# A cross-attention kernel: weights loaded to other buffers, and the work of the first part in another order

## The reference, cut to what matters

```
q    = heads(x @ W_q)                       # x: 4 x 2048 x 640, 20 heads of 32
k, v = heads(text @ W_k), heads(text @ W_v) # text: 4 x 73 x 1024
out  = softmax(q k^T * s) v
k_ip, v_ip = heads(ip @ W_k_ip), heads(ip @ W_v_ip)  # ip: 4 x 4 x 1024
sem  = <l2norm(probs @ text), l2norm(ip)>
out += (softmax(q k_ip^T * s + 0.5 * sem) * mask) v_ip
out  = out @ W_out + b_out + x
```

## Time and profile before

| | |
|---|---|
| median of three runs | 1020.25 us |
| profiled execution, whole | 1022.47 us |
| its span, first to last instruction | 1020.6 us |
| first part, to the barrier | 0 to 88.7 us |
| main loop | 88.7 to 1020.6 us |
| PE busy in the span | 969.2 us (95%) |
| DVE, ACT, POOL busy | 816.6, 695.6, 655.2 us |
| DMA, mean | 177 GB/s |

### The profile page before, as it was taken

One profiled execution on the slowest core, in us unless ns is written; L12 is line 12 of the kernel. 1 busy time (PEld: TensorE's weight loads), 2 busy tenths in 40 slices (PEclk: granted clock), 3 DMA queues, 4 the chain that ended last, 5 costly groups with the idle time before them and its releaser, 6 DMA issues.

```text
span 1020.6 us, 24929 instructions
## 1 busy us (share of the span) xinstructions
PE 969.2 (95%) x7684; PEld 803.6 (79%) x7684; DVE 816.6 (80%) x2409; ACT 695.6 (68%) x2332; POOL 655.2 (64%) x1906
## 2 busy tenths in 40 slices
PE   5987788999999999999999999999999999999988
PEld 5875666888878888888887888888878888888855
DVE  6685698888888887888888888878878888878872
ACT  3534887777776777767776777777667777777740
POOL 3224587776676667677766777676667767776761
PEclk9978999999999999999999999999999999999999
DMA  9936999989889998899899989998899989887973
GB/s 293 298 117 161 195 179 186 177 163 180 168 186 186 186 185 177 163 176 162 174 178 192 192 164 191 169 167 173 167 190 187 180 169 190 137 157 154 149 138 111
DMA packets 488147, 180.27 MB, mean 177 GB/s; under 512 B 449694, under 2 KB 467155, under 8 KB 488015
## 3 DMA queue, kind: packets, MB, share of 16 engines
q1 hardware_dynamic: 487983, 178.63, 86.3%
q10 hardware_dynamic: 32, 0.07, 0.0%
HBM read 42.34 MB, written 27.22 MB: 68 GB/s over the span
## 4 chain that ended last, share of the span: by engine, by line
PE 77%; DMA 5%; DVE 4%; ACT 2%; issue 2%; SPq 2%; POOL 1%; DVEq 0%; ACTq 0%; POOLq 0%
PE ps_O L1257 25%; PE ps_Q L1368 25%; PE ps_S L1278 12%; PE ps_U L1354 11%; DMA pts<-ph 4%; PE ps_M L1294 3%; ACT pr L1038 2%; DMA x_in<-in_x_dram 1%; SPq L951 1%; DVE pr L1199 0%; PE ps_U L1257 0%; DVE n L1211 0%; ACT ph L1050 0%; DVE bias L1160 0%; SPq L924 0%
## 5 line engine op out<-in xcount | busy, mean ns | idle before, releaser
L1038 ACT ACTIVATE pr<-ps_S,bias 128x73 f32<-128x73 f32 x1280 | 288.8, 339 | 101.3 <-DVE bias L1160 100.1
L1120 POOL TENSOR_TENSOR ph<-pr,ph 128x220 f16<-128x220 f32 (+1 forms) x640 | 274.0, 460 | 126.2 <-ACT ph L1050 126.2
L1368 PE MATMUL ps_Q<-xT,wq_hi 128*128 128x512 f32 x800 | 280.1, 415 | 5.2 <-DVE qT L1127 5.2
L1257 PE MATMUL ps_O<-wo_hi,aT 128*128 128x320 f16 x1220 | 279.2, 300 | 0.0
L1050 ACT ACTIVATE ph<-pr 128x292 f16<-128x292 f32 x640 | 241.2, 500 | 0.0
L1257 PE MATMUL ps_O<-wo_lo,aT 128*128 128x320 f16 x610 | 182.3, 299 | 0.0
L1354 PE MATMUL ps_U<-xm,pts 128*128 128x110 f16 (+1 forms) x2560 | 159.3, 212 | 14.9 <-DMA pts<-ph 13.5
L1368 PEld LDWEIGHTS ps_Q<-xT,wq_hi 128*128 128x128 f32 x800 | 146.2, 191 | 32.7 <-DVE qT L1127 6.5
L1354 PEld LDWEIGHTS ps_U<-xm,pts 128*128 128x128 f16 (+1 forms) x2560 | 144.4, 98 | 32.3 <-issue 11.8
L1278 PE MATMUL ps_S<-kbd,qT 128*128 128x308 f32 x960 | 163.0, 304 | 2.6 <-ACT pr L1038 2.1
L1278 PEld LDWEIGHTS ps_S<-kbd,qT 128*128 128x128 f32 x960 | 150.8, 188 | 18.6 <-issue 3.0
(11 more groups left out here) (228 smaller groups left out, 1338.9 us busy)
## 6 DMA issues: line engine op xcount, KB each, us to landing
out_dram<-x_in SPq DMA_DIRECT2D x64, 320.0 KB, 2.6
x_in<-in_x_dram SPq DMA_DIRECT2D x56, 320.0 KB, 3.2
pts<-ph SPq DMA_TRANSPOSE x320, 3.4
w_k<-in_L_xattn_W_k_dram SPq DMA_DIRECT2D x5, 512.0 KB, 8.8
w_ip<-in_L_xattn_W_k_ip_dram SPq DMA_DIRECT2D x1, 2560.0 KB, 11.0
w_v<-in_L_xattn_W_v_dram SPq DMA_DIRECT2D x5, 512.0 KB, 8.3
w_ip<-in_L_xattn_W_v_ip_dram SPq DMA_DIRECT2D x1, 2560.0 KB, 10.6
x_in<-in_x_dram SPq DMA_DIRECT2D x2, 1280.0 KB, 7.2
```

The source lines that it names most:

```text
L1038: last = nc.scalar.activation(pr[p % P_RING][:, j, h, :], sc[:, j, h, 0:T], ACT.Exp, bias=bias[p % 2][:, j, h:h + 1], scale=SCALE)
L1120: nc.gpsimd.tensor_tensor(lo, full[:, :, t0:t1], one[:, :, 0, t0:t1], ALU.subtract).then_inc(pl_ready, 1)
L1257: last = nc.tensor.matmul(bank[:, 0:HALF], stationary, moving, start=(k, a, b_) == O_MMS[0], stop=(k, a, b_) == O_MMS[-1])
L1368: last = nc.tensor.matmul(ps_Q[:], wq[a][:, c, k * P:(k + 1) * P], xT[(CC * i + c) % XT_RING][b_][:], start=(c, a, b_) == Q_MMS[0], stop=( ...
```

## The change

W_q is loaded to a buffer of its own, `w_q`, that lies in the place of `wq_lo`, so that `wq_lo` is computed in place. `w_raw` is then free, and W_out is loaded to it right behind the bias and the mask, with no wait. `ctx_sum` moves from the place of `wq_lo` to the place of the loaded context, `x_in`, and so POOL may only write it once the context's maximum has been taken: the `partition_all_reduce` of that maximum now stands ahead of it. The rest is order.

```diff
-        ctx_sum = nc.alloc_sbuf_tensor_at("ctx_sum", [P, EC, B, T_ALL], F32, offset=g["wq_lo_at"])
+        ctx_sum = g["late0"][:, 0:EC * B * T_ALL].rearrange("p (c b t) -> p c b t", c=EC, b=B)
+        w_q = nc.alloc_sbuf_tensor_at("w_q", [P, CC, C], F32, offset=g["wq_lo_at"])
...
-                sp.dma_start(w_raw[:], g["W_q"].rearrange("(c p) n -> p c n", p=P)).then_inc(ld_wq, 16)
+                sp.dma_start(w_q[:], g["W_q"].rearrange("(c p) n -> p c n", p=P)).then_inc(ld_wq, 16)
...
+                sp.dma_start(w_raw[:], g["W_out"].rearrange("(c p) n -> p c n", p=P)).then_inc(ld_wo, 16)
...
-                sp.wait_ge(wq_hi, 1)
-                sp.wait_ge(wq_lo, 1)
-                sp.dma_start(w_raw[:], g["W_out"].rearrange("(c p) n -> p c n", p=P)).then_inc(ld_wo, 16)
```

More of the change, by code:

```diff
@@ L327, in _ @@
                         key_weights(c + 2)
+                    if c == CC - 2:
+                        act.wait_ge(ld_wq, 16)
+                        nc.scalar.activation(wq[0][:], w_q[:], ACT.Copy).then_inc(wq_hi, 1)
                 value_weights(0)
@@ L339, in _ @@
                                      ACT.Copy).then_inc(k_hi, 1)
[L340 to L345, removed]
                 def value_columns(m):
@@ L364, in value_words @@
                                          ACT.Copy, scale=ss[0:B * GI, 12:13]).then_inc(vw_hi, 1)
+                value_weights(2)
                 value_columns(0)
+                for b in range(B):
+                    act.wait_ge(kg_ready, b + 1)
+                    nc.scalar.activation(kg_raw[:, b, :], ps_S[b % 2][0:T, 0:T_ALL], ACT.Copy).then_inc(kg_read, 1)
+                    if b + 3 < CC:
+                        value_weights(b + 3)
                 act.wait_ge(kg16_ready, 1)
@@ L552, in _ @@
                 link(nc.vector.tensor_scalar(ss[:, 28:29], ss[:, 18:19], 2.0 / 2 ** 14, None, ALU.mult))
+                value_weights(3)
+                value_weights(4)
+                value_max(1)
+                v.wait_ge(vip_parts, 2)
+                nc.vector.tensor_copy(parts[1][:, HALF:C], ps_parts[1][:, 0:HALF]).then_inc(vip_copied, 1)
+                v.wait_ge(wo_hi, 1)
+                nc.vector.scalar_tensor_tensor(out=wo[1][:], in0=w_raw[:], scalar=ss[:, 11:12], in1=wo[0][:],
+                                               op0=ALU.mult, op1=ALU.subtract).then_inc(wo_lo, 1)
+                value_max(2)
                 v.wait_ge(vipt_ready, 1)
@@ L592, in _ @@
                 nc.vector.tensor_scalar(ss[:, 10:11], ss[:, 7:8], float(2 ** 14), ss[:, 24:25], ALU.mult, ALU.min).then_inc(scaled, 1)
-                for n in range(8, 2 * CC):
+                for n in range(4, 2 * CC):
                     words_lo(n)
@@ L682, in _ @@
                 last.then_inc(k_ready, 1)
+                pe.wait_ge(k_lo, CC)
+                values(0)
                 pe.wait_ge(ipt_read, 1)
@@ L705, in _ @@
                 values(3)
+                values(4)
                 pe.wait_ge(vip_read, HG)
@@ L708, in _ @@
                 pe.wait_ge(ld_wo, 16)
-                for n in range(4):
-                    value_words(n)
-                values(4)
-                for n in range(4, 2 * CC):
+                for n in range(2 * CC):
                     value_words(n)
```

66 lines of the change are left out of this document (29 added, 37 removed).

## The result

The changed kernel took **1032.76 us** (median of four runs, 1031.56 to 1033.5) where the kernel before took 1019.5 on the same chip (1017.63 to 1022.09): ratio **1.012**, 95% interval 1.0105 to 1.0135. The forecast was 1014.5 us, and the range ended at 1018.2. The change is slower, and the prediction is wrong in sign. The profiled execution of the changed kernel took 1033.39 us, its span 1031.6, and its barrier fell at 97.8 instead of the forecast 82.9 (88.7 less the gain of 5.8).

The account below looks back on a forecast made before the run. PE's first part, up to the barrier at 88.7 us, was taken to bound the gain, the main loop being unchanged. 5.2 us to the `parts` copy plus 0.6 from the fold on made 5.8: 1020.25 - 5.8 = 1014.5 us, range 1011.8 to 1018.2.

Parts of the forecast that it names:

- stage B: From the context's maximum to the second `parts` copy: `ctx_sum` 33.5 to 39.0, `wv_lo(0)` held 3.1 us, gain 5.2 us.
- my DVE chain: DVE's work from the sum's end at 39.0 to the second `parts` copy: 18.4 us, ending at 57.4, before 62.63.
- the fourth rival: At the late sum on POOL: small scale operations and the PSUM copy on DVE also stand; 1016.2 us, chance 0.08.
- The turns of DVE and POOL: During POOL's eight copies, DVE goes between two ready POOL instructions; waiting for one copy costs 0.5 us.
- POOL didn't keep its turn: Denies the rival that POOL keeps its turn through the eight copies: DVE 3.5 us later, 1018.0 us, chance 0.07.
- Stage A: Up to the context's maximum: `ctx_sum` no longer beside `wk_lo`; PE gains 2.5 us, the maximum comes 1.7 us sooner.
- W_out early: W_out issued at about 33, there by 41, wanted at 45; W_v_ip lands by 50; nothing charged.
- one pause of 2.6: PE's wait before the fold, from about 54.8 to 57.4; the low clock behind it was charged 1.5 us.
- the pause of 4.35 us: PE's wait for the `parts` copy in the kernel before, 58.3 to 62.7; forecast to shrink to 2.6 us.
- the clock doesn't fall: Rival behind PE's pause before the fold: no low clock, or only inside the pause; 1.5 us more gain, 1013.0, chance 0.15.
- The slower rival: From PE's stop at 55 to the barrier the clock stays low: 1030 us, chance 0.04.
- loss 1: In the kernel before, PE waits 1.88 us for a `wk_lo` that stood until POOL's `ctx_sum` was done.

Follow-up runs that it names:

- e1: Changed kernel with the context's sum made by DVE, behind its copy of the first parts, instead of by POOL: 1013.5 us, ratio 0.9926 to the kernel before.
- e2: Changed kernel with the three all-reduces of bias, mask and W_out ahead of the `kbd` casts on POOL: 1023.64 us, ratio 1.0019 to the kernel before.
- e5: e1 with one POOL addition of 128x1 added behind the first all-reduce: 1019.74 us, ratio 0.9989 to the kernel before.
- e6: Kernel before with only the context's sum moved from POOL to DVE, behind the first copy of parts: 1019.83 us, ratio 0.9987.
- e7: Changed kernel with `ctx_sum` on POOL at its old time, in the place of `kbd`; `kbd` cleared and filled behind the all-reduces: 1013.87 us, ratio 0.9933.
- e3: Kernel before with one POOL addition of 128x1 added behind the first all-reduce: 1022.3 us, ratio 0.9998.
- e8: Changed kernel with W_out, and all that SP issues behind it, loaded only after `ctx_sum`: one run of 1030.33 us.
- e9: e1 with both parts of the bias made ahead of the last value columns and the last maximum: 1013.5 us, ratio 0.9928 to the kernel before.
- e4: Kernel before with one POOL copy of 128x1 added behind the first all-reduce: 1021.05 us, ratio 0.999.

## Why the prediction was wrong, point by point

- **The failed step is the first sentence of stage B**: "POOL spreads the maximum (0.5 us from DVE's end to POOL's ...) and then runs `ctx_sum`, 33.5 to 39.0". I costed the two instructions and took nothing for going from one to the other. It took 9.4 us, and since the maximum came 1.8 us sooner than forecast, `ctx_sum` ended 7.6 us late. The extra `ISA` rows stood in the order that I printed, and I read past them. In the kernel before, the one such pair lay in 16.4 us of idle time that was put down to DVE's maximum. The change moves the reduction and the sum out of that cover, and I neither named the cover nor priced its loss. e1, e2 and e5 show it.
- **The second omission, on the same resource**, is the all-reduces behind the casts. In my DVE chain, "W_out's maximum 3.46, Gram scaling 1.45 ... the scale chain 1.5" takes the spread for granted. The all-reduces came 8.2 us after the casts, and DVE stood 6.48 us for them. e2 gave some 10 us back by hiding this.
- **DVE wasn't blocked by the sum**, neither for the 3.1 us of `wv_lo(0)` that stage B has nor for more, as in the fourth rival. `wv_lo(0)` ran at 35.07 in 1.21 us, because the sum hadn't begun. DVE then stood 10.89 us for ACT, which stood for the sum.
- **The sum of the DVE chain was right.** I gave 18.4 us from the end of the sum to the end of the `parts` copy. In e1, with the same instructions in the same order, it is from 37.8 to 55.9, 18.1 us. The turns of DVE and POOL were right too: `wq_lo` took 3.79, 0.3 above, and stands inside the first four casts (6.17 for four, where e2 needed 3.19 for the same four), so each waited for one of the other. POOL didn't keep its turn. In the changed kernel the piece took 24.4 us with the 6.48 of waiting in it, and so 18.0 without; `wv_lo(0)` was no longer part of it.
- **Stage A was right in its mechanism; its worth isn't shown.** The first two `wk_lo` took 2.36 together, and the maximum was over at 31.3, 1.8 us sooner than forecast. The passes took 1.12 us each from 17.54 on, where I had taken 19.3 for the rise of the clock, and PE left the keys at 32.2 instead of 33.1. But e6, where DVE paid 2.7 us for the sum, has the barrier only 1.7 us sooner, and e7 does without the term at the time of e1.
- **W_out early was right**: it was asked for at 33.84, took 9.6 us instead of 7.7 to land, and its maximum was over at 55.9 without a wait. W_v_ip landed at about 50, as forecast, and in e1, where PE came to it on time, PE stood 1.44 us for it. With the 0.55 before the fold that is 2.0 us, where I had one pause of 2.6. That this and the order carry the gain (e7) I had put only indirectly, as the shrinking of the pause of 4.35 us.
- **The clock**: I charged 1.5 us for a pause of 2.6. The pauses were 7.05 and 8.37, and the second was followed by low work of 7.3 us, which cost some 3.2 to 3.6. Of my rivals "the clock doesn't fall" describes e1, where the pause was split in two, 1.44 and 0.55. That its time, 1013.5, is near the 1013.0 of that rival is partly chance: its sum ended at 37.8 and not at 39.0, and its kernel before took 1022.37. From the fold to the barrier e1 took 23.5 us, and my sum without the clock was 24.0.
- **The slower rival was the wrong one.** I had one with its place and price (1030, chance 0.04), a clock that stays low to the end. The time came out near it by another mechanism. The clock was back at full speed at 78.4, before the last group of values.

The Trainium skill, page "GPSIMD Engine Reference", section "2.1 Instruction dispatch", says that the first call to freshly loaded code on GpSimd pays some 6 us, 5.95 as measured there, behind the `MODIFY_POOL_CONFIG` row, without an instruction in the profile that shows it. The rows agree that a pause without an instruction stands behind that row; what fills it no row shows, so that it is a load of code rests on the page. They show it again at each change back, and not only once. On the size they agree in two cases (e3 and e5, 5.7 us to the all-reduce after the addition) and go beyond it in the others, up to 9.7. By an estimate with the page's 6 us at the first of the two places alone, the forecast would have been 1020.5, out of its range.

## What to carry to other kernels

When instructions change places on GpSimd, list the kinds in order and look at each border between them: a switch between the partition all-reduce and a two-input addition cost 6 to 10 us here in either direction, on the path wherever nothing covered it. A copy or a cast adds none of its own, but doesn't save the next one either: the casts between the sum and the all-reduces didn't. Group such instructions, or give the odd one to another engine, even at 2.7 us of a nearly full one. An instruction whose row says 0.38 us and whose idle time is put down to something else may be hiding a load: before moving it, ask what the time ahead of it is covered by.

## What was not expected of the hardware

- The length of the load isn't constant. From the configuration's row to the next instruction it was 9.4 us (changed kernel), 9.7 (e2), 8.9 (e5), 9.1 (e8) and 6.8 (e3) for the addition, and 8.0 (changed kernel), 7.6 (e8), 5.7 (e5) and 5.7 (e3) for the all-reduce. By e8 traffic of the W_out and W_v_ip loads isn't the reason for the 9.4; that of W_v isn't excluded. The tiny addition of e3 and that of e5 are the same instruction and differ by 2.1 us. What makes the difference wasn't found.
- An addition of 128x1 took 0.18 us in e3 and 2.88 in e5. There DVE's `wq_lo`, with two inputs, ran from 39.72 to 43.20, and the addition, started at 40.38, ended at 43.26. It is loss 1 of the prediction with the parts changed: POOL stood until DVE was done.
- A pause of PE of 1.67 us brought the 0.50 level in e6 (ahead of the light Gram products), while one of 1.9 us before the fold in e2 brought none from 60 to 75 us. The length of the pause alone doesn't say whether the level falls.
- The main loop, with the same instructions everywhere, took 929.6 to 934.0 us in the profiled executions (79.06 to 1008.7 in e9, 89.06 to 1023.1 in e4). A forecast of this kernel that carries it over has that much of an error before it begins.
